# A fused post-norm decoder layer: one PSUM bank goes from the row maxima to the small products

## The reference

```python
def _L0_attn_ref(...):          # linear attention, a scan over 512 steps, M = 128
    out_t = einsum('bij,bj->bi', state, q_t)
    state = 0.99 * state + 0.01 * einsum('bi,bj->bij', v_t, k_t)
def _L0_xattn_ref(...):         # cross attention to ctx, 16 heads of 16
    attn = softmax(einsum('bhqd,bhkd->bhqk', qh, kh) / 4)
    out = einsum('bhqk,bhkd->bhqd', attn, vh) ... @ w_o.T + b_o
def _L0_ffn_ref(...):           # self attention, 16 heads of 16, plus a mixture of experts
    attn_out = ...              # softmax attention as above
    gate = softmax(x @ W_gate + b_gate); combine = the two largest of 8
    return attn_out + einsum('bsef,bse->bsf', expert_out, combine)
x = _layernorm(x + _L0_attn_ref(x, ...))
x = _layernorm(x + _L0_xattn_ref(x, ctx_1024, ...))
x = _layernorm(x + _L0_ffn_ref(x, ...))
```

## Time and profile before

| | us |
|---|---|
| median of 3 runs | 1339.93 (1334.83 to 1351.1) |
| the profiled execution | 1342.24 |
| its span, first to last instruction | 1340.5 |
| TensorE busy | 1244.1 |
| VectorE busy | 904.4 |
| ScalarE busy | 776.6 |
| VectorE's reductions to row maxima, 1024 | 657.9 |
| exponentials on ScalarE, 512 | 524.3 |

### The profile page before, as it was taken

The page is one execution under the profiler, slowest core; times in us unless marked ns, Lnnn a source line. Parts: engine busy times, 40 slices in busy tenths (PEclk is TensorE's granted clock), DMA queues, the critical chain, the costliest instruction groups (busy, mean ns, idle before and its releaser), DMA issues.

```text
span 1340.5 us, 19260 instructions
## 1 busy us (share of the span) xinstructions
PE 1244.1 (93%) x6624; PEld 595.3 (44%) x6624; DVE 904.4 (67%) x1808; ACT 776.6 (58%) x1087; POOL 364.9 (27%) x435
## 2 busy tenths in 40 slices
PE   6788989999999999999999999999999999998995
PEld 3333344454444444444444544444444444454442
DVE  5367777566776767766777677766677767667661
ACT  2235555655556655656557566575556566666664
POOL 2300012231622225212333115222252123422162
PEclk9759999999999999999999999999999999998997
DMA  6804424214333134333323343431343333313300
GB/s 226 140 5 71 69 35 62 44 22 80 49 64 63 24 60 64 64 49 48 68 45 50 48 80 49 64 57 24 50 65 48 49 48 42 56 17 48 49 18 17
DMA packets 49841, 74.85 MB, mean 56 GB/s; under 512 B 8521, under 2 KB 20049, under 8 KB 49489
## 3 DMA queue, kind: packets, MB, share of 16 engines
q1 hardware_dynamic: 48736, 73.09, 33.7%
q10 hardware_dynamic: 1008, 0.53, 0.1%
HBM read 18.02 MB, written 4.19 MB: 17 GB/s over the span
## 4 chain that ended last, share of the span: by engine, by line
PE 77%; DVE 9%; issue 5%; ACT 5%; DMA 3%; SPq 2%; POOL 0%; DVEq 0%; ACTq 0%; POOLq 0%
PE ms L411 37%; PE sc L411 14%; PE op L411 13%; PE mx L411 7%; DVE maxes L813 3%; PE ms L430 2%; PE ms L485 2%; DMA qs<-q_parts 2%; DVE k_parts L728 2%; SPq L361 1%; ACT k_parts L605 1%; ACT probs L665 1%; ACT x L683 1%; PE ms L480 1%; DMA qs<-shift_r 1%
## 5 line engine op out<-in xcount | busy, mean ns | idle before, releaser
L813 DVE TENSOR_REDUCE maxes<-mx 128x1 f32<-128x512 f32 x1024 | 657.9, 684 | 343.4 <-PE mx L411 342.5
L665 ACT ACTIVATE probs<-sc 128x1024 f32<-128x1024 f32 x512 | 524.3, 1024 | 452.3 <-PE sc L411 447.7
L974 POOL TENSOR_TENSOR x<-x,moe 128x256 f32<-128x256 f32 x256 | 186.9, 730 | 632.9 <-ACT moe L658 607.8
L411 PE MATMUL op<-probs,v 128*32 128x512 f32 x2048 | 277.0, 613 | 2.2 <-ACT probs L665 1.1
L411 PE MATMUL sc<-qs,ks 50*128 50x512 f32 x1024 | 258.9, 502 | 9.9 <-ACT probs L665 6.6
L411 PEld LDWEIGHTS sc<-qs,ks 50*128 50x128 f32 x1024 | 96.3, 185 | 323.6 <-ACT probs L665 225.2
L411 PE MATMUL mx<-ks,qs 48*128 48x512 f32 x1024 | 210.1, 406 | 14.0 <-DVE maxes L813 12.4
L658 ACT ACTIVATE moe<-ms,comb 128x256 f32<-128x256 f32 x256 | 106.7, 472 | 18.5 <-PE ms L411 18.5
L411 PEld LDWEIGHTS mx<-ks,qs 48*128 48x128 f32 x1024 | 99.2, 190 | 21.9 <-DVE maxes L813 19.1
L411 PE MATMUL ms<-we_hi,x2T_hi 128*128 128x512 f32 x256 | 95.6, 454 | 6.3 <-DVE lin L747 3.5
L411 PEld LDWEIGHTS op<-probs,v 128*32 128x32 f32 x2048 | 40.5, 108 | 95.7 <-issue 94.3
(11 more groups left out here) (104 smaller groups left out, 1192.0 us busy)
## 6 DMA issues: line engine op xcount, KB each, us to landing
ks<-k_parts SPq DMA_DIRECT2D x192, 128.0 KB, 4.7
qs<-q_parts SPq DMA_DIRECT2D x192, 128.0 KB, 5.5
xT_s<-in_xT SPq DMA_DIRECT2D x8, 512.0 KB, 4.8
x_s<-in_x SPq DMA_DIRECT2D x8, 512.0 KB, 4.0
ctxT_s<-in_ctxT SPq DMA_DIRECT2D x8, 512.0 KB, 3.9
out<-x SPq DMA_DIRECT2D x7, 512.0 KB, 2.9
qs<-shift_r SPq DMA_DIRECT2D x128, 8.0 KB
probs<-in_we SPq DMA_DIRECT2D x1, 1024.0 KB, 7.6
```

What stands on the lines that cost most here:

```text
L411: return nc.tensor.matmul(dst, lhsT, rhs, start=first, stop=last, skip_group_check=True)
L665: nc.scalar.activation(probs[:, (2 * s + h) % 3, :, :], sc[:], ACT.Exp).then_inc(exp_out, 1)
L813: nc.vector.tensor_reduce(maxes[:, g % 2, at:at + 1], mx[:, i % 3, :], AX_X, ALU.max).then_inc(max_out, 1)
L974: nc.gpsimd.tensor_tensor(x2[:, n % 2, t, :], x2[:, n % 2, t, :], moe[:, k % 2, j * D:j * D + D], ALU.add).then_inc(acc, 1)
```

## The change

`ms` gets three banks in place of two, `mx` two in place of three; the sum stays. Units take the three banks in turn and wait for the unit three places before. Semaphores `ms_t` and `ms_out`, and the counts that go with them, are per bank and so three each. A maxima pair now uses both banks of `mx`, and so it waits for `max_out` at i, all tiles up to i - 1, in place of i - 1. The instructions and their order are the same on each engine; only banks and waits differ. (One line is added at the top of the file, so lines of the changed kernel are one higher.)

```diff
--- before.py
+++ after.py
@@ -38,6 +38,7 @@
 PHASE = {ph: p for p, ph in enumerate(PHASES)}
 SLOTS = G * TB
 MAX_LEAD = 6
+BANKS, MAX_BANKS = 3, 2
 GROUPS = G * len(PHASES)
 
 LIN_FIRST = {"q1": (-23, 0), "k1": (-23, 1), "v1": (-22, 0), "s0": (-22, 1), "s1": (-21, 0), "s23": (-21, 1),
@@ -153,7 +154,7 @@
     return task in SPLITS or task in ("be0", "be1", "shift", "heads", "gate") or task.startswith("moe")
 
 
-TAKEN = {unit: sum(not own_signal(ORDER[v][0]) for v in range(u % 2, u + 1, 2)) for u, unit in enumerate(ORDER)}
+TAKEN = {unit: sum(not own_signal(ORDER[v][0]) for v in range(u % BANKS, u + 1, BANKS)) for u, unit in enumerate(ORDER)}
 ENTRY = {}
 for unit in ORDER:
     if unit[0].startswith("moe") or unit[0] in ("be0", "be1"):
@@ -272,8 +273,8 @@
                     x2[:].rearrange("p k n d -> p (k n d)"))
 
         sc = ctx.enter_context(nc.psum_tensor("sc", [P, SIDES, 512], F32))
-        mx = ctx.enter_context(nc.psum_tensor("mx", [P, 3, 512], F32))
-        ms = ctx.enter_context(nc.psum_tensor("ms", [P, 2, 512], F32))
+        mx = ctx.enter_context(nc.psum_tensor("mx", [P, MAX_BANKS, 512], F32))
+        ms = ctx.enter_context(nc.psum_tensor("ms", [P, BANKS, 512], F32))
         op = ctx.enter_context(nc.psum_tensor("op", [P, 512], F32))
 
         w_first, w_in, w_late, we_in = sem("w_first"), sem("w_in"), sem("w_late"), sem("we_in")
@@ -281,8 +282,8 @@
         x_in, xT_in, ctx_in, y_out = sem("x_in"), sem("xT_in"), sem("ctx_in"), sem("y_out")
         stack_in = {"k": sem("stack_k_in"), "q": sem("stack_q_in")}
         shift_in = [sem(f"shift_in{n}") for n in range(2)]
-        ms_t = [sem(f"ms_t{n}") for n in range(2)]
-        ms_out = [sem(f"ms_out{n}") for n in range(2)]
+        ms_t = [sem(f"ms_t{n}") for n in range(BANKS)]
+        ms_out = [sem(f"ms_out{n}") for n in range(BANKS)]
         max_t, max_out = sem("max_t"), sem("max_out")
         score, exp_out, pv, oT_out = sem("score"), sem("exp_out"), sem("pv"), sem("oT_out")
         part_high = {"k": sem("k_high"), "q": sem("q_high")}
@@ -301,11 +302,11 @@
         block = ctx.enter_context(nc.Block())
 
         def unit_bank(unit):
-            return ms[:, PLACE[unit] % 2, :]
+            return ms[:, PLACE[unit] % BANKS, :]
 
         def wait_unit(eng, *unit):
 
-            eng.wait_ge(ms_t[PLACE[unit] % 2], PLACE[unit] // 2 + 1)
+            eng.wait_ge(ms_t[PLACE[unit] % BANKS], PLACE[unit] // BANKS + 1)
 
         def wait_unit_out(eng, task, n):
 
@@ -320,7 +321,7 @@
             elif task == "gate":
                 eng.wait_ge(g_step, G_STEPS * n + 1)
             else:
-                eng.wait_ge(ms_out[PLACE[task, n] % 2], TAKEN[task, n])
+                eng.wait_ge(ms_out[PLACE[task, n] % BANKS], TAKEN[task, n])
 
         def half_stack(task, n):
             return 2 * PHASE["S" if "3" in task else "C", n] + int(task[-1])
@@ -433,9 +434,9 @@
             def unit(task, n):
 
                 u = PLACE[task, n]
-                bank = ms[:, u % 2, :]
-                if u >= 2:
-                    wait_unit_out(pe, *ORDER[u - 2])
+                bank = ms[:, u % BANKS, :]
+                if u >= BANKS:
+                    wait_unit_out(pe, *ORDER[u - BANKS])
                 if task in ("q1", "k1"):
                     pe.wait_ge(xT_in, 16 * (n + 1))
                     last = project(bank, W["w" + task], xT_s, slice(0, MEM))
@@ -529,7 +530,7 @@
                             last = mm(bank, x2T_part[i][:, c, t * P:t * P + P].bitcast(F32R),
                                       we_part[j][:, c, 2 * pair * D:2 * pair * D + 2 * D].bitcast(F32R),
                                       m == 0 and c == 0, m == 2 and c == DC - 1)
-                last.then_inc(ms_t[u % 2], 1)
+                last.then_inc(ms_t[u % BANKS], 1)
 
             def max_tiles(i):
 
@@ -539,10 +540,10 @@
                     for name in "kq":
                         pe.wait_ge(stack_in[name], 16 * TERMS * SIDES * (e + 1))
                 if i >= 2:
-                    pe.wait_ge(max_out, i - 1)
+                    pe.wait_ge(max_out, i)
                 for side in range(SIDES):
                     at = 64 * side
-                    mm(mx[:, (i + side) % 3, :], qs[at:at + ROWS, e % RING, 2 * (g % 2) + pair, t * P:t * P + P].bitcast(F32R),
+                    mm(mx[:, (i + side) % MAX_BANKS, :], qs[at:at + ROWS, e % RING, 2 * (g % 2) + pair, t * P:t * P + P].bitcast(F32R),
                        ks[at:at + ROWS, e % RING, 2 * (g % 2) + pair, :].bitcast(F32R), True, True).then_inc(max_t, 1)
 
             def scores(s, h):
@@ -617,7 +618,7 @@
             def take_out(task, n):
 
                 bank = unit_bank((task, n))
-                done = ms_out[PLACE[task, n] % 2]
+                done = ms_out[PLACE[task, n] % BANKS]
                 if task in ("q1", "k1"):
                     if n >= 1:
                         wait_unit(act, "qc1", n - 1)
@@ -810,7 +811,7 @@
                 size = HG * TB
                 at = side * (size // SIDES) + pair * TB + t
                 dve.wait_ge(max_t, i + 1)
-                nc.vector.tensor_reduce(maxes[:, g % 2, at:at + 1], mx[:, i % 3, :], AX_X, ALU.max).then_inc(max_out, 1)
+                nc.vector.tensor_reduce(maxes[:, g % 2, at:at + 1], mx[:, i % MAX_BANKS, :], AX_X, ALU.max).then_inc(max_out, 1)
                 if i % size == size - 1:
 
                     m = maxes[:, g % 2, :].rearrange("p (s m) -> p s m", s=SIDES)
```

## The result

The changed kernel takes 1369.31 us (median of 4 runs, 1367.53 to 1373.66), the kernel before 1341.24 in the same comparison: ratio 1.0203, 95% interval 1.0156 to 1.0251. It is slower by 2.0%; that it is slower is clear of the noise, that it is by more than 2% is not. The forecast of 1371 us was 1.7 us off. The four times of the kernel before spread over 16 us, so a hit that close is partly luck.

What follows compares the result with a forecast made beforehand. TensorE's own order of work was taken as the bound: 64.1 us lost to late pairs less 32.2 us gained, net +31.9 us on the 1339.9 us median, gave 1371 us, range 1353 to 1388.

Steps and rivals of the forecast that it cites:

- 0.22 us per late pair: Second-half maxima pairs wait for the second reduction; units start 0.88 after scores, not 0.66; 56.0 us over h = 1.
- The third bank frees the stalls of the bank kind: Units waiting for the unit two places back no longer wait: 34.9 us, of which 30.5 was counted as gain.
- The slot of moe0 is VectorE's: At moe0, five times, VectorE is the bound, so the 0.60 loss and the 0.88 gain both fall away.
- Nothing else moves: Whole kernel: instruction order on every engine unchanged, no DMA added, semaphore bookkeeping free, granted clock 1.00 in steady stretches.
- Rival D: New waits of about 0.1 us per slot lower the clock; ten slots add some 40 us, 1411; chance 0.03.
- The sum by place: Whole kernel: net +31.9 us; each steady stretch of 32 slots goes from 156.9 to 159.7 us.
- eight waiting pairs of the fill: Before the first scores, eight pairs already waiting on VectorE each lose a whole reduction step, 0.60: 4.8 us.
- Gain and loss as separate prices: Whole kernel: late pairs lose 64.1 us, the third unit bank and absorbed waits give 32.2 us.
- Rivals A: Everywhere, VectorE waits replace each removed bank stall; 64 to 67 us slower, 1404 us; chance 0.08.
- B (the late pair costs half): Every h = 1 pair costs 0.11, not 0.22: +5 us, 1345; chance 0.17 for within 2%, 0.02 for faster.
- rival C: Waits overlap more than counted, remaining data stalls shrink too; up to 15 us off, 1356 us; chance 0.13.
- The signs in the profile: Maxima loads wait 80 to 95 us, low-half waits nearly gone, stretches 159 to 160.5 us, VectorE busy 904.

Runs made afterwards that it cites:

- Three doses of reduction length: The changed kernel with row maxima over 448 or 384 of 512 columns: 1329.09 and 1311.08 us, beside 1369.31 us with all 512.
- the wide gate: The changed kernel with the gate unit's moving tile widened from 8 to 128 columns: 1365.87 us; the kernel before with 384-column maxima, widened likewise: 1323.50 us.
- the maxima part alone: Against the kernel before, two maxima banks and the wait on both tiles, units keeping two banks: 1391.08 us, ratio 1.0356.

## Why the prediction was right, point by point

- **0.22 us per late pair: right.** Load 0.45 and units 0.88 behind the scores were forecast; 0.46 and 0.89 stand in the slot above, and in 217 of 246 h = 1 halves the first unit starts 0.83 to 0.95 behind the scores. Three doses of reduction length confirm the formula (below 0.23 nothing, then one for one).
- **The third bank frees the stalls of the bank kind: right.** q3c0 is shown; in the kernel before 33 first units start 1.05 or 1.32 to 1.33 behind their scores, and all 33 start at 0.88 to 0.89 now. The operand waits of hT0 and x0 stayed and absorbed the late pair: hT0 starts 2.04 behind the scores (583.91, 585.95) as before (580.70 - 578.66).
- **The slot of moe0 is VectorE's: right.** Pair load 648.61 against scores 646.96, 1.65, and moe0's matmuls 0.43 later at 649.04.
- **Nothing else moves: wrong in one point.** Falls of the clock at gate units, four with 1.3 to 1.6 us each, some 6 us; by the mean granted clocks of the two profiles (0.965 over 1365.7 us, 0.972 over 1340.5) at most 10 us in all, an estimate as above. Rival D had falls of the clock at 3% and 40 us, through the new waits. Falls came, with a sixth of that size, but not by those waits. The Trainium skill (TensorE: Matmul & The Clock Gate, A second HAM failure mode: psum-queue depth-cycling) describes a kernel that swings between the levels by small idles between its groups; here the falls follow a unit that is busy without a pause, with 8 columns to a matmul, and the wait of 0.1 us in each slot brought none by itself: the stretch from 331 to 490 us has a late pair in all 32 slots and a clock of 1.00, and so have four stretches with the wide gate.
- **The sum by place: errors against each other.** Forecast: +31.9 in all and +2.8 for a stretch, so five stretches leave 17.9 for start and end. Measured: +28.1 between the medians and +25.3 between the profiled spans. There slot 48 starts at 330.97 in place of 330.13, +0.8; a stretch without a fall is +2.2, with one +3.6 to 3.9, and the fifth, also with a fall, +4.2; from slot 208 (1111.38 before, 1130.00 after) to the end it is +6.7. So start and end gave 7.5 in place of 17.9, and the falls, which were not in the sum, gave some 6 back. That the total came so near is luck to this extent. The term that was mis-sized is the start: eight waiting pairs of the fill at 0.60 and the first-half pairs. The kernel with the maxima part alone is 13.1 us behind at slot 48 (343.19), so the price of the late pairs is real there, but the third bank then gives back more than was counted. Beside it the clock's low times lie differently in each profile (slot 48 starts at 335.89 in the wide-gate kernel, whose waits are the same), so the start isn't settled to better than some 5 us.
- **Gain and loss as separate prices: both too large.** The maxima part alone costs 49 us, not 61 to 65, and the third bank is worth 22, not 30. The prediction's sum was made for both at once, in which each half-slot counts the 0.22 and the stall together, and there it holds; taken one by one they overlap. Rivals A (the bank gives nothing) and B (the late pair costs half) are both out by these runs. The misses of the sum, 2.2 in place of 2.8 us in a stretch without a fall and the smaller start, go the way of rival C (waits in each other's shadow, up to 15 us less); no run tests that it is this.
- **The signs in the profile: nearly all.** The maxima loads wait 97.1 us in 273 waits, where 80 to 95 in about 250 were named; the stretches are 159.2 to 160.8 us at clocks of 1.00 and 0.99, where 159 to 160.5 at 1.00 were, the excess being the falls.

## What to carry to other kernels

Ask for each buffer not how long its readers take but how late the release comes behind the moment at which the writer would come anyway: here 0.23 us of lateness were free, and 0.22 more were charged to the path in nearly every h = 1 half. Two changes with opposite signs at the same place have to be priced together, because alone each hides in the other's wait. A small matmul group can be cheap next to one neighbour and dear next to another: behind the scores the pair adds 0.22 us, and moved into a unit to hide a wait it cost more than the wait (67 us in all, up to 27 of them the clock's).

None of the exact variants beat the kernel before. The kernels with maxima over part of the columns did (1311 us with three unit banks, 2.4% under before). The maximum only shifts the exponent and cancels in the softmax, but a score far above the partial maximum is then not held down, so this trades a safety of the kernel and was used as a probe.

## What the runs showed of the hardware

- A weight load of a pair that comes late costs 0.42 to 0.43 us to the next group, with one matmul or with two; right behind the scores the same pair adds 0.22 (units at 0.66, at 0.44 without it).
- Where a unit follows scores with no pair between, or follows a pair inside a unit, 0.44 us pass from the 48- or 50-row weight load to the next 128-row one, with nobody to wait for; a second such step makes the half-slot shown 0.40 longer.
- VectorE takes 0.55, 0.62, 0.68 and 1.23 us for a maximum over 384, 448, 512 and 1024 columns of PSUM, and starts on two banks at once 0.52 behind the matmul where it starts on one 0.43 behind.
- A release by VectorE reaches the waiting weight load in 0.05 to 0.06 us (610.07 to 610.13 in the slot above).
- Sixteen matmuls of 8 columns take 1.95 us and sixteen of 128 columns 2.05. A fall of the granted clock begins within 4 us of the start of 43 of 96 narrow groups and of none of 16 wide ones.
